# Attention phase of a fused kernel: side products move from the spare PSUM banks to the score banks, products with the values run up to five blocks behind

## What is computed

```python
x_ln = layer_norm(x_flat, g1, beta1)               # (16, 1024, 64)
q, k, v = split(x_ln @ w_qkv.T, 3)                 # 8 heads of 32 channels
scores = einsum('bhqd,bhkd->bhqk', q, k) * 32 ** -0.5
attn = softmax(scores, axis=-1)
out = einsum('bhqk,bhkd->bhqd', attn, v)           # then a projection, a feed-forward layer and three more blocks
```

## Time and profile before

| What | us |
|---|---|
| median of three runs (3671.5 to 3675.89) | 3671.86 |
| span of the profiled execution | 3666.4 |
| first and last exponential of the attention phase start at | 104.9 and 1973.5 |
| one mid period | 58.19 |
| in such a period busy: PE / POOL / DVE / ACT | 55.26 / 45.31 / 44.63 / 37.58 |

### The profile page before, as it was taken

How to read it: one execution, slowest core, us unless ns; L and a number is a source line. 1 busy time by engine, 2 the same in 40 slices (tenths; PEclk the granted TensorE clock), 3 DMA queues, 4 the chain that set the end, 5 groups by cost and what they waited for, 6 DMA issues and landing times. The chain is left out here.

```text
span 3666.4 us, 55668 instructions
## 1 busy us (share of the span) xinstructions
PE 3163.0 (86%) x18550; PEld 1183.9 (32%) x18550; DVE 2573.4 (70%) x3346; ACT 2006.1 (55%) x2381; POOL 2214.4 (60%) x684
## 2 busy tenths in 40 slices
PE   6999999999999999999995899774888888887787
PEld 2333333333333333333331233341322222222222
DVE  5777777777767777777771222142888988988988
ACT  3566666666656666666663333223555564565554
POOL 0577777777777777777776000003657666666666
PEclk7899999999999999999998999886989999999999
DMA  2000000000000000000003211114333433443443
GB/s 103 12 16 10 16 16 16 16 13 16 16 17 10 16 16 16 19 10 16 16 10 74 92 69 46 48 64 149 119 132 128 155 142 120 153 150 118 147 150 115
DMA packets 74739, 234.86 MB, mean 64 GB/s; under 512 B 13088, under 2 KB 14180, under 8 KB 74420
## 3 DMA queue, kind: packets, MB, share of 16 engines
q1 hardware_dynamic: 69460, 215.06, 17.3%
q0 software_dynamic: 5056, 16.83, 1.3%
HBM read 192.42 MB, written 39.39 MB: 63 GB/s over the span
## 5 line engine op out<-in xcount | busy, mean ns | idle before, releaser
L526 DVE TENSOR_REDUCE at_pmax<-at_ring 128x1 f32<-128x512 f32 x2048 | 1300.8, 685 | 392.0 <-PE at_ring L334 381.2
L479 ACT ACTIVATE at_probs<-at_sc 128x1024 f32<-128x1024 f32 x1024 | 992.5, 1021 | 531.7 <-PE at_sc L402 529.7
L580 POOL TENSOR_TENSOR at_prob_sums<-at_prob_sums,at_probs 128x2048 f32<-128x2048 f32 x256 | 1159.0, 4527 | 74.8 <-ACT at_probs L479 54.5
L398 PE MATMUL at_sc<-at_QT,at_KT 32*128 32x512 f32 x4096 | 782.5, 634 | 4.1 <-issue 3.7
L1634 POOL TENSOR_TENSOR ss_drive<-ss_du,ss_bsb 128x1024 f32<-128x1024 f32 x261 | 610.7, 2352 | 263.9 <-DVE ss_state L1591 257.1
L1534 ACT ACTIVATE ss_decay<-ss_delta,ss_a 128x512 f32<-128x512 f32 x520 | 354.5, 687 | 447.6 <-DVE ss_state L1587 299.5
L410 PE MATMUL at_O<-at_probs,at_V 128*32 128x512 f32 x4096 | 535.3, 606 | 52.5 <-DVE at_att L549 51.6
L580 POOL TENSOR_TENSOR at_prob_sums<-at_probs 128x2048 f32<-128x2048 f32 x64 | 290.7, 4543 | 403.1 <-ACT at_probs L479 403.1
L1423 PE MATMUL ss_Y<-ss_seen,ss_ident 128*128 128x512 f32 x1032 | 520.7, 628 | 0.0
L334 PE MATMUL at_ring<-at_KH,at_QH 32*128 32x512 bf16 x2048 | 442.3, 387 | 5.7 <-DVE at_pmax L526 2.9
L1599 DVE TENSOR_TENSOR ss_seen<-ss_state,ss_C 128x1024 f32<-128x1024 f32 x259 | 316.3, 1221 | 80.4 <-PE ss_C L1411 72.6
(11 more groups left out here) (199 smaller groups left out, 2695.6 us busy)
## 6 DMA issues: line engine op xcount, KB each, us to landing
ss_bsb<-scratch_rows SPq DMA_DIRECT2D x265, 512.0 KB, 6.9
scratch_attn<-at_att SPq DMA_DIRECT2D x64, 256.0 KB, 2.0
fc_att<-scratch_attn SPq DMA_DIRECT2D x32, 512.0 KB, 5.8
ss_xn<-scratch_xm SPq DMA_DIRECT2D x34, 256.0 KB, 5.6
at_xn<-scratch_xn SPq DMA_DIRECT2D x32, 256.0 KB, 3.8
ss_xw<-scratch_xw SPq DMA_DIRECT2D x17, 256.0 KB, 3.9
ln_x<-in_x SPq DMA_DIRECT2D x8, 512.0 KB, 4.2
scratch_xn<-ln_xn POOLq DMA_DIRECT2D x8, 512.0 KB, 3.0
```

The lines of the kernel that those rows point to most:

```text
L398: nc.tensor.matmul(sc[:, h, :], KT[head(h), par, blk(kb)], QT[head(h), par, hs(half)], start=True, stop=False)
L479: nc.scalar.activation(probs[:, kb, two, :].rearrange("p h q -> p (h q)"), sc[:, two, :].rearrange("p h q -> p (h q)"), ACT.Exp, scale=SCA ...
L526: nc.vector.tensor_reduce(pmax[:, quad // 2, h, quad % 2:quad % 2 + 1], ring[:, unit[3], :], AX_X, ALU.max, negate=True).then_inc(max_done, 1)
L580: nc.gpsimd.tensor_tensor(prob_sums[:, half, :, :], before, probs[:, k, :, :], ALU.add).then_inc(pool_sums, 1)
```

## The change

**Where side products land.** Denominators, turns and projections no longer use the ring. They are written to the score banks, between the exponential of one step and the scores of the next: q and k of half 0 into pair 0 and of half 1 into pair 1 at step 0; turn into bank 0 and denominators into bank 1 at steps 3 and 11; v into pair 1 at step 11. PE waits for the exponential of the step before it writes them (`wait_for_scores`), and the scores of the next step wait for ACT's reading (`wait_for_pair`, semaphore `extra_done`). The ring holds maxima only: 64 in a period, with the bank (4 s + h) % 3.

**When they are made.** The denominators go from steps 1 and 9 to steps 3 and 11, the turns from 4 and 12 to 3 and 11, v from step 6 to 11, and all four q and k products stand in step 0.

**Values.** They run four to five blocks behind, by the table `VALUES_AT`; there are none in steps 4 and 12, and two blocks in steps 5 and 13. The last period ends with four blocks in a row instead of one.

**ACT and DVE.** ACT copies q and k of a half in one instruction over two banks, makes the bfloat16 copies (in steps 1 and 2) instead of DVE, and copies v in one instruction. DVE keeps the maxima and the normalisation, which moves from steps 2 and 10 to steps 5 and 13.

```diff
+    EXTRA = [(0, "qk", 0), (0, "qk", 1), (3, "turn", 1), (3, "den", 1),
+             (11, "turn", 0), (11, "den", 0), (11, "v", 0)]
+
+    VALUES_AT = {0: [12], 1: [13], 2: [14], 3: [15], 5: [0, 1], 6: [2], 7: [3], 8: [4], 9: [5], 10: [6], 11: [7],
+                 13: [8, 9], 14: [10], 15: [11]}
...
+    def slot(s, h):
+        return (s * GH + h) % SLOTS
...
             def maxima(stage, grp, par, s, heads):
...
                 if quad == 0 and heads[0] == 0:
-                    pe.wait_ge(cast_done, 4 * (grp + later) + 4)
+                    pe.wait_ge(cast_done, 2 * (grp + 2))
                 for h in heads:
-                    unit = unit_of(stage, "max", h, s)
-                    wait_for_bank(stage, grp, unit)
...
+                    before = same_slot_before(stage, grp, s, h)
+                    if before:
+                        pe.wait_ge(max_done, max_count(*before))
...
+            def wait_for_scores(grp, s, n):
+
+                pe.wait_ge(exp_done, 2 * (STEPS * grp + s) + n + 1)
...
+                if stage != "lead":
+                    wait_for_scores(grp, 0, half)
+                for n in range(2):
...
+                    m = nc.tensor.matmul(sc[:, 2 * half + n, :], w[rows, at:at + P], xn[rows, hs(half)], start=True, stop=True)
+                m.then_inc(extra_ready, 1)
...
+            def wait_for_pair(stage, grp, s, n):
+
+                if s > 0:
+                    wait_for_scores(grp, s - 1, n)
+                elif stage != "first":
+                    wait_for_scores(grp - 1, STEPS - 1, n)
...
+                last = {(1, 0): ("qk", 0), (1, 1): ("qk", 1), (4, 0): ("den", 1), (12, 0): ("den", 0), (12, 1): ("v", 0)}.get((s, n))
...
+                if last and made(stage, *last, s):
+                    pe.wait_ge(extra_done, extra_count(stage, grp, *last))
...
                     maxima(stage, grp, par, s, (0, 1))
...
+                    if stage != "lead":
+                        for n in VALUES_AT.get(s, []):
+                            if n < s:
+                                values(grp, par, n)
+                            elif stage != "first":
+                                values(grp - 1, 1 - par, n)
+                    if s == 0:
+                        project(stage, grp, par, 0)
+                        project(stage, grp, par, 1)
+                    if s == 3:
+                        turn(stage, grp, s, 1)
+                        denominators(stage, grp, s, 1)
+                    if s == 11:
+                        turn(stage, grp, s, 0)
+                        denominators(stage, grp, s, 0)
                         values_projected(stage, grp, par)
...
                     maxima(stage, grp, par, s, (2, 3))
...
+                nc.scalar.activation(QK[:, 1 - par, :, hs(half)], sc[:, pair(half), :], ACT.Copy).then_inc(extra_done, 1)
...
+                nc.scalar.activation(QKH[:, 1 - par, :, hs(half)], QK[:, 1 - par, :, hs(half)], ACT.Copy).then_inc(cast_done, 1)
...
-                    if s == 2 and stage not in ("lead", "first"):
+                    if s == 5 and stage not in ("lead", "first"):
                         normalise(grp - 1, 1)
-                    if s == KB + 2 and stage != "lead":
+                    if s == 13 and stage != "lead":
                         normalise(grp, 0)
```

More of the change, by code:

```diff
@@ L172, in executed @@
         return not (stage == "first" and kind == "den" and which == 1)
[L174 to L186, removed]
+    STAGES = ("lead", "first", "mid", "last")
+    EXTRAS = {stage: [u for u in EXTRA if made(stage, u[1], u[2], u[0])] for stage in STAGES}
+    MAXIMA = {stage: [(s, h) for s in range(STEPS) for h in range(GH) if made(stage, "max", h, s)] for stage in STAGES}
+    def slot(s, h):
+        return (s * GH + h) % SLOTS
     def stage_before(stage, grp):
@@ L191, in stage_before, with counted_before, extra_count, max_count @@
         return "first" if isinstance(grp, int) and grp == 1 else "mid"
-    def counted_before(n, grp):
+    def counted_before(units, grp):
         if isinstance(grp, int) and grp <= 0:
[L196 to L212, removed]
+            return len(units["lead"]) * (grp + 1)
+        return len(units["lead"]) + len(units["first"]) + len(units["mid"]) * (grp - 1)
+    def extra_count(stage, grp, kind, which):
+        return counted_before(EXTRAS, grp) + [u[1:] for u in EXTRAS[stage]].index((kind, which)) + 1
+    def max_count(stage, grp, s, h):
+        return counted_before(MAXIMA, grp) + MAXIMA[stage].index((s, h)) + 1
+    def same_slot_before(stage, grp, s, h):
+        at = MAXIMA[stage].index((s, h))
+        for u in reversed(MAXIMA[stage][:at]):
+            if slot(*u) == slot(s, h):
+                return stage, grp, *u
         if stage == "lead":
@@ L215, in same_bank_before @@
         was = stage_before(stage, grp)
[L216 removed]
+        return was, grp - 1, *[u for u in MAXIMA[was] if slot(*u) == slot(s, h)][-1]
     with ExitStack() as ctx:
@@ L257, in head, with pair @@
             return slice(h * DH, (h + 1) * DH)
[L259 to L263, removed]
+        def pair(n):
+            return slice(2 * n, 2 * n + 2)
         def image_loop(eng, period):
@@ new lines, in turn, with reciprocals @@
+            def turn(stage, grp, s, half):
+                if not made(stage, "turn", half, s):
+                    return
+                act.wait_ge(extra_ready, extra_count(stage, grp, "turn", half))
+                nc.scalar.activation(nrow[:, half, :], sc[:, 0, :], ACT.Copy).then_inc(extra_done, 1)
+            def reciprocals(of, count):
+                act.wait_ge(extra_ready, count)
+                if of is not None:
+                    act.wait_ge(rden_done, of)
+                nc.scalar.activation(lden[:], sc[:, 1, :], ACT.Ln).then_inc(extra_done, 1)
+                if of is not None:
+                    act.wait_ge(od_free, of)
@@ L464, in reciprocal, with denominators @@
                 act.wait_ge(extra_done, count)
                 nc.scalar.activation(rden[:], lden[:], ACT.Exp, scale=-1.0).then_inc(rden_done, 1)
+            def denominators(stage, grp, s, half):
+                if not made(stage, "den", half, s):
+                    return
+                reciprocals(None if stage == "first" else 2 * (grp - half) + half, extra_count(stage, grp, "den", half))
             def period(grp, par, stage):
@@ L501, in period @@
[L501 to L507 removed]
+                        for n in range(2):
+                            act.wait_ge(sc_ready, 2 * (STEPS * grp + s) + n + 1)
+                            nc.scalar.activation(probs[:, kb, pair(n), :].rearrange("p h q -> p (h q)"),
+                                                 sc[:, pair(n), :].rearrange("p h q -> p (h q)"), ACT.Exp,
+                                                 scale=SCALE).then_inc(exp_done, 1)
```

218 lines of the change are left out of this document (86 added, 132 removed).

## The result

The changed kernel takes 3738.28 us (3735.02 to 3747.69), the kernel before beside it 3673.88 (3671.5 to 3679.56): a ratio of 1.0181, 95% interval 1.0164 to 1.0198. The forecast was 3696 with a range up to 3728, so the sign was right and the size too small by 42 us. The profiled executions last 3734.1 and 3666.4; their difference of 67.7 is accounted for here.

The account below looks back on a forecast made before the run. A loop between PE and ACT sets the pace of plain steps. The period goes from 58.19 to 58.98 us; 31 x 0.79 = 24.5, ends zero, makes 3691 profiled and, with 5.5 added, 3696; range 3660 to 3728.

Parts of the forecast that it names:

- the values ahead of the turn: Steps 3 and 11: a block of values was priced at 0.85 us on PE before the turn starts.
- The walk: One attention period followed step by step with trace prices: 58.98 us against 58.19, trusted to 0.4 us a period.
- The wrap: Step 0: its first maximum shares bank 0 with step 15's last, holding values and all behind on PE by 0.60 us.
- the hand-back of v: Step 12: pair 1 waits for ACT's copy of v until 45.48; the cost is about 1.2 us.
- the two-bank copies: On ACT: a copy over two banks was taken as 1.02 us, with 0.60 and 1.20 as the ends.
- `lden` at step 4: Start of step 4: ACT's `lden` holds bank 1, so the scores start 0.78 us late.
- the normalisation at step 13: Step 13: DVE normalises until 50.04, so values start at 50.09; `at_O` should wait more here than at step 5.
- Moved work that costs nothing: Whole period: POOL's sums end in time, ACT rises some 1.5 us to 39, and SP's stores hold nobody long.
- The ends: Attention phase's lead and end: three more value blocks (2.6 us) against four fewer DVE copies, together zero within 3 us.
- Slower still: Rival: copies at 1.20 lengthen steps 1, 3 and 12 and block step 2, 0.6 to 1.2 together; 3715 to 3733; chance 0.14.
- Faster: Rival: score banks come back unnoticed, so 2.6 us a period falls away, 56.4, or 3615 us; chance 0.12.
- The reasoning on step 12: Step 12: maxima are reported behind pair 1's bias, making it near 3.7 us; reported by themselves, the period is about 58.1.

Follow-up runs that it names:

- the first run: Changed kernel with only the ring banks' numbering shifted by one behind the second product of step 3: 3763.47 us, 1.0266 times the kernel before.
- the run with both blocks doubled: Changed kernel with block 15 of the values multiplied a second time in step 4 and block 7 in step 12: 3710.02 us, 1.0104 times the kernel before.
- the shorter end: Kernel with moved blocks, shifted numbering and earlier normalisation, plus values catching up in the last period: 3639.89 us, 0.9916 times the kernel before.
- the control: The changed kernel as it is, run again on the same chip as three of the follow-ups: 3740.49 us, 1.0186 times the kernel before.

## Why the sign was right and the size wrong

Two terms of the sum failed: the clock, which had no term, and the values ahead of the turn, which were sized too small.

- **The walk held.** The forecast steps 0, 1, 2, 4, 5 and 6 to 15 but for 11 came within 0.2 us, and so did the steps that the single edits were to move, but for the copies back on DVE. The wrap (0.60, the first run) and the hand-back of v (the run with v in step 7) were shown by their removal; the two-bank copies cost 1.02 and 1.01, as taken. The waits came where they were forecast: in a plain period PE stands idle 0.18 for DVE at the first maximum of step 0, 0.47 for `lden` at step 4 and 0.73 for the normalisation at step 13, and not for it at step 5.
- **A term mis-sized: the values ahead of the turn.** The 0.85 came from values followed by values. Ahead of the turn they cost 1.00, in steps 3 and 11. With the later start of the values in step 3 (0.16), the later `lden` (0.08), and v's place behind the denominators (0.14 and 0.07) this makes 0.39 and 0.36, against the 0.37 and 0.31 by which the two steps were walked too short. The other steps miss by -0.19 together, which leaves the period's 0.49: 31 x 0.49 = 15 us of the 42.
- **A term that was not there: the clock.** This is the step that failed most. The sum priced PE's work at the granted clock of 1.00 in the earlier trace rows. "Moved work that costs nothing" named the covers of POOL, ACT and SP, but not what a step without values does to PE. This was some 19 us in the periods, net of what the kernel before loses in the same way, and, by the last period of the run with both blocks doubled, about 5 more: the two largest parts of the 42 are the clock's 24 and the steps' 15.
- **The ends, taken as zero within 3.** The lead gained 3.1. The last period lost 5.6, nearly all clock. From the first exponential of its step 15 on another 6.1 were lost, but that stretch lies between 1689.6 and 1703.8 in all runs here with no order in it, so no cause is read from it; the shorter end made no difference that can be told.
- **The rivals.** "Slower still" named nearly the right time, 3715 to 3733, by the wrong mechanism: no copy was dearer. "Faster" fell; the hand-backs are met each time. The reasoning on step 12 stood: it is 3.58 with v's hand-back and 2.46 without. As in the earlier trace rows, the maxima there start ahead of the bias of pair 1 and are reported behind it. The sentence that the prediction took from the Trainium skill ("PSUM — Partial Sum Buffer", "Engine vs sequencer instructions") has products start in program order too; there the profile's start times differ, since the bias is the older of the two in the code.

## What to carry to other kernels

When products move, look for steps that the move leaves without their large products, and price them at both levels of the clock: here two empty steps cost as much as the mechanism that was walked, and filling them made the kernel faster even with useless work. A walk through single steps came within 0.2 us of every step but two and then showed the better order: one block in every step. A saving tried alone can come out negative and still be right, as the ring's numbering did.

## What the hardware showed that was not expected

- The granted clock fell to 0.50 for some 7 us after a step with scores and maxima only, although PE was shown busy for 2.47 of 3 us, and not at an idle time of 0.79 behind a step with values. At the wait of 0.82 in step 6 of the kernel before it fell in one of the mid periods. Shortening the period by 0.6 without filling the steps made the stretches more frequent, from one in three periods to nearly all.
- A copy from SBUF to SBUF on DVE does not end while a sum runs on POOL: it took 0.69 alone, 2.59 and 3.65 beside POOL, and the sum that began before the copy's end took 4.83 for 4.52. The Trainium skill, "SBUF — State Buffer", section "SBUF: two separate sides", says that the port pair shared by the two is locked for a whole instruction; the trace agrees, and the copies from the ring in the kernel before, which read PSUM, ran at 0.69 beside the same sums. Leaving these copies to ACT was worth 296 us against the control, more frequent stretches at half clock among them.
- Products of values took 1.00 us ahead of the bfloat16 turn and 0.85 ahead of more values.
